# A graph, attention and mixture-of-experts layer on one core: layer-2 side rows copied by ScalarE and added by GpSimd, the shared expert's up products first, one down matrix loaded during the row scatter

## The reference, cut to what matters

```python
xn = _layernorm(x)
x = x + gnn(xn) + mix(xn)          # mix: linear attention over all rows, then w_proj
x = x + ffn(_layernorm(x))

# gnn
out1 = gat_conv(layer_norm(xn), ..., H=4, C=192)      # layer 1
out2 = gat_conv(out1, ..., H=2, C=96)                 # layer 2
return concatenate([xn, out2]) @ Wu + bu

# gat_conv, for each head: h = x @ W
e = leaky_relu(s_src[src] + s_dst[dst], 0.2)
alpha = exp(e - segment_max(e)) / segment_sum(...)
out = segment_sum(alpha * h[src], dst) + bias

# ffn: two of eight experts for each row
routed = sum over the two of gate * (silu(x @ w_gate[e]) * (x @ w_up[e])) @ w_down[e]
shared = silu(x @ ws_gate) * (x @ ws_up) @ ws_down
return sigmoid(x @ sg_w + sg_b) * shared + (1 - sigmoid(...)) * routed
```

## Time and profile before

| | |
|---|---|
| Median of 3 runs | 1595.71 us (1594.91 to 1598.98) |
| Profiled execution, own time | 1598.5 us |
| Its span, first to last instruction | 1596.8 us |
| Mean granted TensorE clock | 0.988 |
| Busy: PE / DVE / ACT / POOL | 1524.4 / 824.9 / 329.6 / 450.4 us |
| Graph layers 1 and 2 | about 486 to 842 us of the span |
| Shared expert | about 873 to 1015 us |
| Expert tiles | 1017 us to the end |

### The profile page before, as it was taken

The page is one execution under the profiler, slowest core; times in us unless marked ns, Lnnn a source line. Parts: engine busy times, 40 slices in busy tenths (PEclk is TensorE's granted clock), DMA queues, the critical chain, the costliest instruction groups (busy, mean ns, idle before and its releaser), DMA issues.

```text
span 1596.8 us, 21967 instructions
## 1 busy us (share of the span) xinstructions
PE 1524.4 (95%) x8300; PEld 1001.8 (63%) x8301; DVE 824.9 (52%) x1526; ACT 329.6 (21%) x481; POOL 450.4 (28%) x466
## 2 busy tenths in 40 slices
PE   5999999999999899999989997999999999999996
PEld 3566676558889899999886554444444444444442
DVE  8655457886678799876987142212122222221221
ACT  3321121112240445640671110100000000000000
POOL 1187865653300000000000047032232333232322
PEclk9999999999999999999999999999999999999998
DMA  9900010000034427114203247915619322613451
GB/s 260 363 2 2 2 63 1 1 1 1 1 81 131 108 57 210 35 22 103 61 1 97 112 97 169 303 51 198 220 48 337 101 55 54 207 50 116 154 201 26
DMA packets 83372, 163.81 MB, mean 103 GB/s; under 512 B 19979, under 2 KB 61185, under 8 KB 80730
## 3 DMA queue, kind: packets, MB, share of 16 engines
q1 hardware_dynamic: 55383, 119.07, 23.0%
q0 software_dynamic: 12096, 23.27, 6.6%
q10 hardware_dynamic: 15810, 20.41, 5.0%
HBM read 127.75 MB, written 37.56 MB: 104 GB/s over the span
## 4 chain that ended last, share of the span: by engine, by line
PE 80%; DVE 10%; issue 3%; DMA 3%; POOL 1%; ACT 1%; SPq 0%; ACTq 0%; DVEq 0%; POOLq 0%
PE bank L828 34%; PE bank L1722 6%; PE bank L1683 6%; PE bank L1585 5%; PE bank L1498 5%; PE bank L1642 5%; PE bank L1470 4%; PE bank L738 3%; DVE arena L2453 2%; PE bank L1523 2%; DVE arena L2422 2%; DMA expert_in<-arena 2%; DVE arena L2398 2%; PE bank L1770 2%; POOL expert_in L694 1%
## 5 line engine op out<-in xcount | busy, mean ns | idle before, releaser
L828 PE MATMUL bank<-arena 128*64 128x384 f32 x3312 | 544.7, 487 | 0.6 <-ACT arena L916 0.6
L828 PEld LDWEIGHTS bank<-arena 128*64 128x64 f32 x3312 | 233.9, 137 | 287.3 <-issue 286.4
L1722 PE MATMUL bank<-arena 125*125 125x198 f32 (+1 forms) x1200 | 192.4, 321 | 12.1 <-DVE arena L2422 11.9
L1722 PEld LDWEIGHTS bank<-arena 125*125 125x125 f32 x1200 | 186.1, 196 | 16.3 <-DVE arena L2422 16.2
L1188 DVE TENSOR_TENSOR arena<-bank,arena 128x384 f32<-128x384 f32 x46 | 25.7, 558 | 302.0 <-PE bank L828 302.0
L1683 PE MATMUL bank<-arena 128*125 128x192 f32 x960 | 164.0, 329 | 0.6 <-DVE arena L2375 0.6
L1683 PEld LDWEIGHTS bank<-arena 128*125 128x125 f32 x960 | 157.7, 189 | 0.9 <-DVE arena L2375 0.9
L1376 POOL TENSOR_SCALAR arena<-arena 128x125 bf16<-128x125 f16 x186 | 115.4, 623 | 111.6 <-PE bank L1523 106.8
L1370 POOL DMA_INDIRECT slot_table<-arena x80 | 112.0, 1400 | 93.8 <-issue 93.8
L2261 DVE TENSOR_TENSOR arena<-arena,bank 125x417 f32 x186 | 109.8, 590 | 52.1 <-PE bank L1523 43.4
L717 POOL TENSOR_TENSOR arena<-arena 64x768 f32<-64x768 f32 x44 | 79.6, 1808 | 185.3 <-DMA arena<-out_dram,arena 141.6
(11 more groups left out here) (310 smaller groups left out, 1663.6 us busy)
## 6 DMA issues: line engine op xcount, KB each, us to landing
arena<-in_L_ffn_w_gate_dram SPq DMA_DIRECT2D x9, 2304.0 KB, 10.0
arena<-in_L_ffn_w_up_dram SPq DMA_DIRECT2D x9, 2304.0 KB, 10.8
arena<-in_L_ffn_w_down_dram SPq DMA_DIRECT2D x9, 2304.0 KB, 9.9
arena<-score_rows ACTq DMA_DIRECT2D x18, 585.9 KB
expert_in<-arena SPq DMA_DIRECT2D x23, 384.0 KB, 10.5
arena<-expert_in ACTq DMA_DIRECT2D x92, 96.0 KB, 2.4
arena<-in_L_mix_w_qkv_dram SPq DMA_DIRECT2D x2, 2304.0 KB, 17.5
xn_columns<-arena SPq DMA_DIRECT2D x1, 3750.0 KB, 15.3
```

The costliest lines, as they stand in the source:

```text
L828: ins = tp.matmul(ps[bank][HP * h:HP * h + HP, 0:384], frm[:, b, k, HP * h:HP * h + HP], ew[h][i][:, k, n * 384:(n + 1) * 384], start=(k = ...
L1722: ins = tp.matmul(ps[bank][0:T, c * width:(c + 1) * width], ptile[0:T, j % NPT, dt * T:(dt + 1) * T], values(n - first, st), start=(st == ...
```

## The change

- **Side rows of layer 2.** 28 of the sides (all of layer 2 but the two at its start and the two at its end) are no longer added by VectorE. ScalarE copies each from PSUM into `xrow` and signals `s_fe`; GpSimd adds it to `x2` and signals `s_sideadd`. The places of the sides in layer 2 and the maxima are dealt out anew: ten sides before the first rows of layer 2 are turned and seven after, nine in the steps of its first head and two in the second; eight maxima of the second head ahead and two in the loop.
- **Scores of layer 2.** For head 4 the broadcast no longer goes through DRAM: TensorE turns each score column, broadcast, into a PSUM bank, and ScalarE copies three pieces into `srowb[0]`. Head 5's still goes through DRAM. The turn of the score rows uses bank 4.
- **Score row 2 of layer 1** is read two steps into head 0 instead of right after its rows.
- **Shared expert.** All ups first, then turns and downs in turn. The hidden rows are written in place over the silu results, downs use four banks (2, 3, 6, 7), and the first expert rows are turned into banks 0 and 1 before the last down.
- **DMAs.** SyncE, not ScalarE, loads the first expert rows. Its order is now: down of expert 7 once the ups are done (while rows are scattered), wait for the rows, the first rows, gate and up of expert 7, the slot information, down of expert 0 once the hidden rows are turned, all output rows.

```diff
@@ planning
-        SIDE_START2 = (3, 7, 8, 9)
+        SIDE_START2 = (2, 0, 10, 7)
         def side_layer2(h, st):
-            return ((0, 1, 1, 1, 0, 0, 0, 0, 0, 0), (0,) * 10)[h][st]
+            return ((0, 1, 1, 1, 1, 1, 1, 1, 1, 1), (1, 1, 0, 0, 0, 0, 0, 0, 0, 0))[h][st]
+        ACT_SIDES = sum(SIDE_START2[1:]) + sum(side_layer2(h, s) for h in range(H2) for s in range(NT))
+        ACT_FIRST = 2 * NF - SIDE_END - ACT_SIDES
-        AHEAD = 6
+        AHEAD1, AHEAD2 = 6, 8
...
-                    (0,) * 10, (0, 1, 1, 1, 1, 0, 0, 0, 0, 0), (0,) * 10)[n][st]
+                    (0,) * 10, (0, 1, 1, 0, 0, 0, 0, 0, 0, 0), (0,) * 10)[n][st]
@@ SyncE
-            for t in range(2):
-                store_rows(t)
+            sp.wait_ge(s_sup, NT)
+            load_expert(1, 2)
             sp.wait_ge(s_rows, 16 * 2 * NT)
+            for i in range(4):
+                sp.dma_start(xgb[32 * i:32 * i + 32, 0], xg_dram[32 * i:32 * i + 32]).then_inc(s_xg[0], 16)
...
             load_expert(1, 0)
-            for t in range(2, 4):
-                store_rows(t)
-            sp.wait_ge(s_sup, NT)
             load_expert(1, 1)
-            load_expert(1, 2)
-            sp.wait_ge(s_sh, NT)
-            load_expert(0, 2)
-            for t in range(4, NT):
-                store_rows(t)
             sp.wait_ge(s_info, 16 * 2 * NT)
...
+            sp.wait_ge(s_shT, NT)
+            load_expert(0, 2)
+            for t in range(NT):
+                store_rows(t)
@@ GpSimd
+            for u in range(ACT_FIRST, ACT_FIRST + ACT_SIDES):
+                t, c = u % NT, CHUNKS[u // NT]
+                if t == 0 or u == ACT_FIRST:
+                    pool.wait_ge(s_x[c], 64)
+                pool.wait_ge(s_fe, u + 1)
+                pl.tensor_tensor(x2[0:T, t, c], x2[0:T, t, c], xrow[0:T, u % NX], ALU.add).then_inc(s_sideadd, 1)
@@ TensorE, shared expert
-            for t in range(3, NT):
-                shared_up(t)
-                shared_turn(t - 2)
-                shared_down(t - 3)
...
+            for t in range(NT):
+                if t + 1 < NT:
+                    shared_turn(t + 1)
+                if t == NT - 1:
+                    first_x_transposes()
+                shared_down(t)
@@ TensorE, start of layer 2
+            for i, (a, m) in enumerate(PIECES):
+                for d in range(m):
+                    ins = tp.transpose(ps[i][0:T, d * T:(d + 1) * T], s2rows[0:T, a + d:a + d + 1].to_broadcast([T, T]), ident[0:T, 0:T])
+                ins.then_inc(s_spread, 1)
             turn_rows(S2, s2rows[0:T])
@@ ScalarE
             for t in range(NT):
-                if t == 6:
-                    act.wait_ge(s_rows, 16 * 2 * NT)
-                    load_first_x()
-                    load_x(1, 1)
                 act.wait_ge(s_shT, t + 1)
...
-                if n + 2 < H1:
+                if 0 < n < H1 - 2:
                     score_row(n + 2)
...
+            def take_sides(n):
+                for _ in range(n):
+                    u = sides_taken[0]
+                    act.wait_ge(s_f, u + 1)
+                    if u == ACT_FIRST:
+                        act.wait_ge(s_fe, u)
+                        act.wait_ge(s_x[0], 64)
+                    if u >= ACT_FIRST + NX:
+                        act.wait_ge(s_sideadd, u - ACT_FIRST - NX + 1)
+                    sc.activation(xrow[0:T, u % NX], ps[side_bank(u)][0:T, 0:FW], ACT.Copy).then_inc(s_fe, 1)
+                    sides_taken[0] = u + 1
...
             def aside2(h, st):
+                if h or st > 1:
+                    take_sides(side_layer2((h * NT + st - 2) // NT, (st - 2) % NT))
...
+            act.wait_ge(s_big, H1 - 1)
+            for i, (a, m) in enumerate(PIECES):
+                act.wait_ge(s_spread, i + 1)
+                sc.activation(srowb[0:T, 0, a * T:(a + m) * T], ps[i][0:T, 0:m * T], ACT.Copy).then_inc(s_srow[0], 1)
             take_rows(S2)
-            for h in range(H2):
-                score_row(H1 + h)
-            heads(H2, H1, aside2)
+            score_row(H1 + 1)
+            heads(H2, H1, aside2, lambda i: take_sides((SIDE_START2[1] + SIDE_START2[2], SIDE_START2[3] - 1, 1)[i]))
@@ VectorE
-            shared_h(2)
             dve.wait_ge(s_exout, 2)
-            for t in range(3, NT):
+            for t in range(2, NT):
                 shared_h(t)
-                shared_out(t - 3)
...
+            for t in range(NT):
+                shared_out(t)
...
+            taken[0] += ACT_SIDES
+            dve.wait_ge(s_fe, taken[0])
             take_sides(SIDE_END)
+            dve.wait_ge(s_sideadd, ACT_SIDES)
```

More of the change, by code:

```diff
@@ L500, in gps_layer @@
         SIDE_START1 = (0, 0, 11, 9)
+        SIDE_END = 2
         def side_layer1(h, st):
@@ L2434, in largest_next @@
                             dst_rows(n)
[L2436 removed]
+                take_own_sides(start_units[1])
                 for dt in range(NT):
                     if dt > 1:
[L2439 removed]
+                        take_own_sides(1)
                     largest_next(1)
[L2441 to L2442 removed]
+                take_own_sides(start_units[2] - (NT - 2))
+                for i in range(ahead(first)):
                     largest_next(1)
                     if i:
[L2445 removed]
+                        take_own_sides(1)
                 for n in range(first, first + H):
```

103 lines of the change are left out of this document (55 added, 48 removed).

## The result

The changed kernel takes 1583.35 us (median of 7 runs, 1582.05 to 1585.75), the kernel before 1595.16 (7 runs beside them, 1589.60 to 1598.98). The ratio is 0.9924, with a 95% interval of 0.9906 to 0.9943: faster by 11.8 us, 0.8%. The forecast was 1575 and 20 us; the range of 1563 to 1585 holds the result, the forecast's own range of 1571 to 1580 doesn't. The profiled execution took 1583.85 us around a span of 1582.1.

A forecast was written before the change was run, and what follows sets the result against it. TensorE works nearly all the span, so gains come from its gaps or the slow matmuls behind them. Terms 2.5 + 10.5 + 8 = 21 us give 1577.5 from the profiled 1598.5, 1574.7 off the median: forecast 1575, range 1563 to 1585.

The forecast's parts named there:

- Step (1): Layer 1: later broadcast of score row 2 lets stores land earlier, shrinking TensorE's gap; 2.5 us, bounds -1 to +6.
- Steps (2) and (3): Layer 2, start and head loop: first head product at 757.5, last at 827.9; together 10.5 us, bounds 4 to 14.
- the sentence on what stands in ScalarE's list: Layer 2: lowerings and exps queue behind ScalarE's new waits on sides; with 2.7 us work per 4.1 us step it stays ahead.
- "blocked" rival: Layer 2: GpSimd's adds and VectorE's passes exclude each other; (2, 3) give only 3 us, 1582; chance 0.09.
- Step (4): Shared expert to tile 0: waits and slow matmuls go, gate matrix late by 2.5 to 3 us; gain 7.5 to 8.
- slower rival: Expert tiles: output stores at 4.3 us a tile hold VectorE, and 1575 becomes 1597; chance 0.03.
- no head start: Layer 2: ScalarE's waits on sides in front of the row store hold everything, no gain there, 1585; chance 0.04.

The follow-up runs named there:

- the part alone: One part of the change put by itself into the kernel before: layer-2 part 1592.82 us, shared expert's part 1587.88 us.
- sides_first: Changed kernel with ScalarE issuing the score-row broadcast of layer 2's second head after six sides, not before the first: 1576.92 us.
- both_moves: Changed kernel with the edits of sides_first and gate_between together: 1575.40 us.
- early_down: both_moves with TensorE entering tile 0 after 18 of VectorE's 20 additions, and expert 0's down matrix issued before the slot-information loads: 1577.87 us.
- matrix_behind: Changed kernel with the second expert's down matrix loaded after the scatter, behind its gate and up matrices: 1588.98 us.
- loads_behind: Kernel before with ScalarE's wait for scattered slot rows and its eight loads moved behind its ten shared-expert copies: 1596.61 us.
- gate_between: Changed kernel with the second expert's gate matrix issued between the slot rows of tile 0 and tile 1: 1581.98 us.
- small_adds: sides_first with each of GpSimd's 28 additions cut from 192 columns to 4: 1579.52 us.

## Why the prediction was right or wrong

It was right in the sign and in the range, by 1.65 us at the range's upper end, and its 20 us came out as 11.8.

**Step (1), 2.5 us, measured 0.15 in the trace and nothing in the time.** The term was mis-sized. The first gap did shrink: 3.04 to 3.34 us in three of the four traces with the old place of score row 2 and 2.73 in the fourth, 0 to 2.98 in the ten with the new one. But the step took the gap as time won for the layer. The sides and products behind it are not the bound there; VectorE is, which works without a pause from 527.16 until the addition that TensorE waits for at 549.30. And the clock's loss was not kept or won but moved, from the first product to the fourth.

**Steps (2) and (3), 10.5 us, measured 4.8 in the pair of traces and 3.2 by the medians of the part alone.** The step that failed is the sentence on what stands in ScalarE's list. I looked at what the new waits on sides would hold up behind them, and made a rival of it, and did not look at what would hold up the sides: the broadcast of head 5, with its wait for the landing of the row store. It cost 4.27 us of standing and 2.6 of clock. With that one step moved (sides_first), layer 2 wins 10.4 us (over all traces: 126.1 us in the mean of five with the stall, 119.8 of three without it (sides_first, both_moves, early_down), 130.3 of four with the old layer 2, so 4.2 and 10.5), the rows are turned when the prediction said, and the first head product starts at 39.3 us behind the spreading, 39.7 being the forecast (757.5 - 717.8). GpSimd's additions took 1.05 us in the mean and not 0.75, inside the bounds of 0.35 to 1.81:

```profile
L699 POOL TENSOR_TENSOR arena<-arena 125x192 f32<-125x192 f32 x28 | 29.2, 1047 | 344.1 <-ACT arena L2017 344.1
```

The "blocked" rival was right in its mechanism and wrong in its consequence: the maxima did stretch, to 1.77 us, which the prediction had named as a sign of being wrong, but VectorE's rows were ready at 735.8, one microsecond later than worked out, still ahead of the tenth side. That its 1582 lies next to the measured 1583 is chance.

**Step (4), 8 us, measured 8.2 by the medians of the part alone and 10.2 in the pair of traces.** The size was right. TensorE was ready for tile 0 when the prediction said (998.2, plus the 4.9 us that it came in earlier: 1003.1, against 1003.5), and the gate matrix was late as said, but by 2.03 us instead of 2.5 to 3, and the clock cost 1.7 us instead of 3.2. The scatter's end, taken 1.8 us later, did not move in this pair of traces. The slower rival never came near: 20 store issues took 20.12 us, and VectorE had its output rows at 1032.7 and went on to tile 1's hidden rows at 1038.4, without holding TensorE. What the step missed without harm is that the down matrix beside the scatter is a gain (5.6 us, matrix_behind) and that the wait it counted as won, 8.15 us, isn't won by taking it away alone (loads_behind).

The chances were too bold in one place: all the cases were built around the terms as worked out, and none was "an old wait in front of new work", which is what happened ("no head start" had the order the other way round, new waits in front of the row store). Only the width kept it in the range, and that is luck.

## What to carry to other kernels

When an engine is given new work in the middle of its list, list both what the new waits will hold up and which old waits now hold up the new work; a DMA that the engine stores and then reads back is the first place to look: its landing took 8.1 us here, and the three side banks were full after 6.0. A wait that ends with a burst of transfers isn't priced by its own length: take it away and the next consumer may wait for transfers of the same burst (loads_behind), so look at who needs which of them first, and move out of it what can go ahead. One trace of each kernel isn't enough to price a part whose wait ends on such transfers: the stretch with the old shared expert differed by 7.6 us between three traces. And when a late transfer is mended, look at the other operands of the same instruction: here VectorE's last addition lay 0 to 3.5 us under the matrix (tile 0 starts 160.2 us behind the output product in the three traces where this addition ends the wait, and 160.2 to 163.7 in the four where the matrix does), and in gate_between it hid the gain of the earlier matrix.

## What the runs showed of the hardware

A GpSimd addition of 125 x 192 float32 takes 0.54 us alone and 1.67 when a VectorE pass with two operands in SBUF has begun just before it (the longest of the 28 in the changed kernel took 2.48); a pass goes from 1.45 to 1.77 us. I had expected to find this on the path, and it wasn't.

Eight loads of 96 KB landed in 4.2 us (median) at the head of the queue (changed kernel). In loads_behind the first of them were there about 16 us after ScalarE asked for them, 9 us behind a 2.3 MB matrix that SyncE had asked for: asking from another engine's list didn't let them pass.

A gap of TensorE before expert tile 0 of 1.65 us kept the granted clock, and the 84 instructions took 13.77 us; gaps of 2.03 and 3.26 us cost 1.7 us behind them, both the same, and one of 5.09 us (small_adds) 2.0. Before the first head product of layer 1 the length of the gap alone didn't decide: 2.98 us (early_down) kept the clock, 2.74 us (matrix_behind) lost it, with products of 3.62 and 5.30 us.
